# Inverse transform ahead of the next pair's forward transform on TensorE, in a fused cross-attention and feed-forward kernel

## The reference

```python
Q = (layernorm(x) @ wq) ; K = (ctx @ wk) ; V = (ctx @ wv)      # 16 heads of 16
corr = irfft(rfft(Q, axis=-1) * conj(rfft(K, axis=-1)), n=L)   # along the sequence
top_vals, top_idx = top_k(corr, 4) ; w = softmax(top_vals)
out = sum_i w[i] * take(V, (t - top_idx[i]) % 16, along the head dimension)
x = x + out @ wo
# feed-forward, weights as 8-bit integers, x and hidden as 16-bit integers with one scale each
x = x + quantized(gelu(quantized(layernorm(x)) @ W_in + b_in)) @ W_out + b_out
```

## Time and profile before

| | |
|---|---|
| median of 3 runs | 1052.65 us (1051.55 to 1053.36) |
| the profiled execution's own time | 1051.32 us |
| its span on the core | 1049.5 us |
| TensorE busy | 1016.4 us, 97% |
| VectorE busy | 985.6 us, 94% |
| ScalarE busy | 885.8 us, 84% |
| GpSimd busy | 514.6 us, 49% |
| granted TensorE clock, mean | 0.998 of full speed |

### The profile page before, as it was taken

The page is one execution under the profiler, slowest core; times in us unless marked ns, Lnnn a source line. Parts: engine busy times, 40 slices in busy tenths (PEclk is TensorE's granted clock), DMA queues, the critical chain, the costliest instruction groups (busy, mean ns, idle before and its releaser), DMA issues.

```text
span 1049.5 us, 30279 instructions
## 1 busy us (share of the span) xinstructions
PE 1016.4 (97%) x9870; PEld 760.5 (72%) x9870; DVE 985.6 (94%) x2836; ACT 885.8 (84%) x1573; POOL 514.6 (49%) x742
## 2 busy tenths in 40 slices
PE   7999999999999999999986999999999999999998
PEld 5788888888888888888865444444444888888887
DVE  4999999999999999999987999999997999999998
ACT  4677888888888888888867788888888999999996
POOL 6889999999999999999964200000001000000000
PEclk9999999999999999999999999999999999999999
DMA  6544433444445444444421598999989999999995
GB/s 193 166 138 132 156 126 135 129 130 131 130 133 166 132 143 134 131 130 132 131 72 52 172 337 300 313 312 298 299 300 358 358 359 347 360 354 353 344 365 195
DMA packets 145305, 226.89 MB, mean 216 GB/s; under 512 B 76321, under 2 KB 87713, under 8 KB 141089
## 3 DMA queue, kind: packets, MB, share of 16 engines
q1 hardware_dynamic: 144368, 224.59, 63.3%
q10 hardware_dynamic: 816, 0.79, 0.2%
HBM read 121.26 MB, written 83.89 MB: 195 GB/s over the span
## 4 chain that ended last, share of the span: by engine, by line
PE 71%; ACT 2%; DVE 1%; issue 1%; SPq 1%; POOL 1%; DMA 0%; DVEq 0%; ACTq 0%; POOLq 0%
PE sums L685 21%; PE bank L654 11%; PE sums L654 11%; PE sums L488 5%; PE sums L501 4%; PE bank L533 4%; PE sums L558 4%; PE bank L574 4%; PE sums L519 3%; PE bank L545 3%; PE sums L691 1%; SPq L338 1%; SPq L378 0%; PE bank L519 0%; DMA arena<-in_x_turned 0%
## 5 line engine op out<-in xcount | busy, mean ns | idle before, releaser
L685 PE MATMUL sums<-wout,arena 128*128 128x256 f16 x2048 | 229.8, 273 | 1.2 <-DVE arena L1568 1.2
L685 PEld LDWEIGHTS sums<-wout,arena 128*128 128x128 f16 x2048 | 197.0, 98 | 32.4 <-DVE arena L1561 7.3
L1568 DVE SCALAR_TENSOR_TENSOR arena<-arena,wout_rel 128x512 f16<-128x512 int16 x256 | 180.4, 746 | 2.0 <-ACT arena L951 0.9
L654 PE MATMUL sums<-arena,win 128*128 128x512 f16 x512 | 115.9, 379 | 1.1 <-DVE arena L1513 0.9
L654 PE MATMUL bank<-arena,win 128*128 128x512 f16 x512 | 115.7, 379 | 0.0
L1532 DVE TENSOR_REDUCE hmax_all<-arena 128x1 f32<-128x1024 f32 x96 | 111.2, 1211 | 2.9 <-ACT arena L908 2.9
L1129 POOL CAST store_x<-one 128x1 bf16<-128x1 f32 x1 | 0.2, 189 | 220.0 <-DVE one L1550 220.0
L951 ACT ACTIVATE arena<-arena,wout_rel 128x512 f16<-128x512 int16 x159 | 106.2, 706 | 0.0
L908 ACT ACTIVATE arena<-sums,b_in_sb,z_scale 128x512 f32<-128x512 f32 x128 | 97.4, 778 | 9.8 <-PE sums L654 5.1
L944 ACT ACTIVATE arena<-arena,one 128x1536 int16<-128x1536 f32 x63 | 99.2, 1575 | 4.5 <-DVE arena L1568 3.0
L501 PE MATMUL sums<-store_x,arena 128*128 128x256 f16 x768 | 94.3, 272 | 2.8 <-ACT arena L705 2.0
(11 more groups left out here) (152 smaller groups left out, 2350.3 us busy)
## 6 DMA issues: line engine op xcount, KB each, us to landing
hidden_scratch<-arena SPq DMA_DIRECT2D x32, 1536.0 KB, 5.5
arena<-hidden_scratch SPq DMA_DIRECT2D x64, 768.0 KB, 6.8
arena<-in_ctx_turned SPq DMA_DIRECT2D x64, 256.0 KB, 2.9
arena<-in_x_turned SPq DMA_DIRECT2D x64, 256.0 KB, 3.3
arena<-in_x SPq DMA_DIRECT2D x64, 256.0 KB, 3.6
x_scratch<-arena SPq DMA_DIRECT2D x64, 256.0 KB, 3.4
arena<-x_scratch SPq DMA_DIRECT2D x32, 512.0 KB, 5.8
out<-arena SPq DMA_DIRECT2D x31, 512.0 KB, 4.4
```

The source lines that it names most:

```text
L654: last = nc.tensor.matmul(bank[f][:, :].rearrange("p (n t) -> p n t", n=4), win16[:, f, c, :], xt[q % 3][:, s, :, c, :], start=s == 0 and ...
L685: last = nc.tensor.matmul(bank[m * 2 + k // 2][:, k % 2 * D:(k % 2 + 1) * D], gbuf[:, s, f, k * P:(k + 1) * P], wout16[:, f, :], start=f = ...
L1568: V.scalar_tensor_tensor(gbuf[:, 1, f, :], hq[:, f, :], wout_rel[:, f:f + 1], gbuf[:, 0, f, :], ALU.mult, ALU.subtract).then_inc(S["c_lo"], 1)
```

## The change

In the loop of TensorE's `step(t)`, `inverse(t-1)` is issued ahead of `transform(t)` and no longer behind it. No instruction is added or taken away, no wait is changed, and the other engines keep their order. The order behind the loop, for the last two pairs, stays as it was.

```diff
@@ -603,10 +603,10 @@
                     project_out(t - 4)
                 if active(t, 3):
                     attend(t - 3)
+                if active(t, 1):
+                    inverse(t - 1)
                 if active(t, 0):
                     transform(t)
-                if active(t, 1):
-                    inverse(t - 1)
 
             for t in range(PAIRS - 2):
                 step(t)
```

## The result

The changed kernel takes 1065.51 us (median of 4 runs, 1064.20 to 1066.11), the kernel before 1052.72 in the 4 runs beside it. The ratio is 1.012, with a 95% interval of 1.0105 to 1.0135: slower by 12.8 us, where 13.3 were forecast.

What follows compares the result with a forecast made beforehand. TensorE's own work of 8.36 us set a plain step before; the new loop through ScalarE sets it after. Stretches of -0.7, +12.1 and +1.6 and +0.3 behind the loop sum to +13.3: 1066.0 us, range 1059 to 1073.

Steps and rivals of the forecast that it cites:

- first stretch: 16 steps from the transform of t = 5 to that of t = 21: 136.0 us against 136.74, -0.7.
- second stretch, weight steps: 24 steps from t = 21 to 45, one extra ScalarE weights instruction each: 8.93 us a step, +12.1 in all.
- Point 1: TensorE's inverse, now right after `attend`, doesn't wait; its earlier result gains VectorE's `top_values` 0.
- Point 2: TensorE's transform starts 1.10 us later, so its first-stretch waits for VectorE's `mix_q` go: at most 1.4 us gained.
- Points 3 and 4: Later transform delays ScalarE's `take_q`, `squares`, `take_k`, then `project_q`; this closes a loop of 8.46 us a plain step, against 8.36.
- Point 5: ScalarE's weights instruction between `take_q` and `squares` enters the loop in 24 steps: 0.47 us on average, 8.93 a step.
- Point 6: VectorE's `products` falls 0.27 us behind, hidden in the loop; GpSimd's `minus_mean2` ends about when ScalarE is ready; 0.3 once behind.
- Point 7: New neighbours at TensorE's boundaries between matmul kinds cost 0 a step; bounds 0.1 less or more, -5.6 to +5.6 us.
- Loads drawn ahead: Rival: the inverse's first weight load is done under `attend`'s matmuls, gaining 0.1 us a step: 1060.3 us; chance 0.15.
- dearer boundaries: Rival: TensorE's two new boundaries cost 0.1 us more a step, or 0.2: 1071.6 us or beyond; chance 0.13.
- The rival that ScalarE swallows the delay: No change: plain steps stay at 8.36 us, the second stretch moves within 2 us: 1051 to 1055; chance 0.06.
- Faster: Rival: only the transform's freedom from waiting for `mix_q` counts, first stretch loses its 3.0 us excess: 1049.6 us; chance 0.04.

Runs made afterwards that it cites:

- the run in halves: Kernel before with the inverse cut in two, four matmuls ahead of the transform and four behind it: 1058.90 us, ratio 1.0066.

## Why the prediction was right

The balance of the profiled executions, +14.8 us against the +13.3 forecast:

| part | forecast | measured |
|---|---|---|
| up to the transform of t = 5 | 0 | 55.81 - 55.49 = +0.3 |
| first stretch | -0.7 | +1.1 |
| second stretch, weight steps | +12.1 | 213.62 - 202.17 = +11.5 |
| third stretch, plain steps | +1.6 | 135.44 - 133.72 = +1.7 |
| behind the transform of t = 61 | +0.3 | 521.57 - 521.38 = +0.2 |

Part of the nearness is luck. The medians differ by 12.8 us and the two profiled executions by 14.8, on either side of the forecast. The first stretch came out 1.9 above its forecast and the second 0.6 below. And the hit in the last row is luck: the mark of the table, the transform, stands 1.09 us later in its step, so the first row holds 1.09 us that the last gives back. Without them the start gained 0.8 and the part behind the loop lost 1.3, where 0 and 0.3 were forecast. Neither figure is clear of how these parts vary: the first transform of all starts between 14.0 and 15.1 us in the eleven traces, and what lies behind that of t = 61 takes 521.4 to 522.9 us in the three kernels with TensorE's old order and no delay. The granted clock there was at its lower level, 1.2 GHz, for 3.4 us in the kernel before and for 6.8 in the changed one. The upper end of the range was added up from 1071.6 and 2.3, which is 1073.9 and was written as 1073; nothing hangs on it.

Point 1 held: the inverse waits nowhere between the transforms of t = 5 and 61, and coming early brings VectorE nothing that shows.

Point 2 held, and I had looked too short. The waits of the transform for `mix_q` go from the loop; ahead of t = 5 they were 5.1 us in 5 places and are now 1.6 in one. In the changed kernel the transform stands 1.09 later in its step, and yet that of t = 5 starts only 0.3 later, so the fill gained 0.8 (counted from the first transform on, which starts 0.5 later there for no reason of the change, 1.2). I had costed the fill at nothing.

Points 3 and 4 are what set the time. The forecast times after the transform (`take_q` 1.19, `take_k` 3.04, `project_q` 3.76) were measured at 1.20, 3.04 and 3.77, and the plain step at 8.46 to 8.47 for 8.46. The two moves of `take_k` and the delays on ScalarE show the cause from both sides: taking `squares` out of the loop removes the loss, and putting a delay of 1.00 us into it with the old order brings 9.5 us of loss about in the weight steps, where the change lost 11.5.

Point 5 held with its size off by 0.03: the weights' instructions cost 0.40 and 0.52 us, not 0.43 and 0.55, so steps are 8.86 and 8.98. I had taken the overlap of two instructions as 0.09 and it is 0.11. This is most of the 0.6 us by which the second stretch came out below its forecast.

Point 6 held for TensorE in plain steps but was too simple about GpSimd. I had written that `minus_mean2` would end "about where ScalarE is ready". In the first stretch, where VectorE has more to do, it comes later than that in every other step. Here lies the only term with the wrong sign, -0.7 for +1.1. The run with `minus_mean2` moved shows 1.2 of the 1.9 us of the difference; that the rest is GpSimd's too is read from the starts of `squares`, not tested. VectorE itself waits for `take_q` in weight steps (L1286 stands idle for 10.0 us in 22 of the 24 steps of the second stretch and starts 2.25 after the transform in them). That wait comes from the longer steps and doesn't make them: with `take_k` first, `take_q` comes as late after the transform, VectorE waits for nothing in that stretch and starts L1286 only 2.58 to 3.78 after the transform, and the kernel is fast; with the delay on ScalarE alone, `take_q` keeps its old time and the weight steps are long.

Point 7, the boundaries: 0 a step, as taken. The two rivals on them fell. Loads drawn ahead would have shown as fewer than 0.98 us from `attend` to inverse, and dearer boundaries as more; it was 0.99. Half of the first rival did come true: the 0.41 us in which the inverse's weight load stood idle are gone. But the same 0.41 us now stand ahead of the load of `project_k`, 23.0 us in the 56 steps before and after. They go with what follows the transform, and the swap only changes what that is. The rule of the Trainium skill ("TensorEngine Tiling (Array Packing)", Key Properties) that a change of tiling mode drains TensorE agrees with the run in halves, where one change more cost 0.20 us, and with the changed kernel, where their number stayed.

The rival that ScalarE swallows the delay failed by 0.10 us in plain steps and by 0.50 and 0.62 in weight steps. "Faster" is what the change would be without the loop: with `take_k` ahead of `squares` it comes to 0.9979, 1050.05 us. That this rival gave 1049.6 is chance, since it took its 3.0 us from the first stretch, which was 136.57 us in that run and 136.74 before.

## What to carry to other kernels

When two independent pieces swap places on the bound engine, look at who waits for the one that moves back, and follow that engine's own queue: what stands behind the waiting instruction there, up to whatever the bound engine wants from it. The slack to compare with is the idle time on that queue, step kind by step kind, since 11.5 of the 14.8 us here lay in 24 of 56 steps, 9.6 of them by one extra instruction. If such a loop closes, reordering the other engine's queue (the instruction that the bound engine waits for first, the others behind) can be worth more than the swap either way.

## What the runs showed that I had not expected

TensorE can lose 0.11 us in every step and still be printed as busy for 135.44 of 135.44 us, because the modelled end of a matmul group lies 0.16 us behind the next group's usual start; the distance between starts is what to read. One more change between a 64 x 128 and a 64 x 32 group cost 0.20 us a step, where the widest distance inside the old order had let me think of 0.1. And ScalarE instructions from SBUF into 16-bit SBUF, 0.316 us long by the group's mean at 128 columns, followed each other every 0.20 us, while those of 0.51 us at 256 columns were followed after 0.40: the overlap is about 0.11 us in both, so it is a larger share of a short instruction, and many short copies delay the queue by less than their printed lengths add up to.
